# Turning quantised rows by DMA instead of TensorE in a Mamba block with a ternary MLP

## What is computed

```python
x = x + tanh(g_xattn[0]) * mamba(ctx_1024, z=layernorm(x), ...)
x = x + tanh(g_ffn[0]) * ffn(layernorm(x), w1, w2, w3)

def step(state, inp):                      # over the 512 rows, 512 channels x 16 states
    dA = exp(d[..., None] * A)
    state = state * dA + (d * u)[..., None] * b[:, None, :]
    return state, einsum('bdn,bn->bd', state, c)

def bitlinear(x, w):                       # w: -1, 0, 1 times a scale; x: 8-bit integers times a scale of the row
    xn = rmsnorm(x)
    return einsum('bsi,oi->bso', activation_quant(xn), weight_quant(w))

h = silu(bitlinear(x, w1)) * bitlinear(x, w2)      # 2048 wide
out = bitlinear(h, w3)
```

## Time and profile before

| | us |
|---|---|
| median of 3 executions | 655.52 |
| lowest, highest | 654.02, 656.09 |
| the profiled execution, its own time | 653.69 |
| its span (first to last instruction) | 651.9 |
| busy: POOL, DVE, ACT, PE, PEld | 587.9, 583.0, 530.7, 488.3, 296.4 |
| time of the 16 DMA engines in the SP queue's packets | 33.9% |

### The profile page before, as it was taken

The page is one execution under the profiler, slowest core; times in us unless marked ns, Lnnn a source line. Parts: engine busy times, 40 slices in busy tenths (PEclk is TensorE's granted clock), DMA queues, the critical chain, the costliest instruction groups (busy, mean ns, idle before and its releaser), DMA issues.

```text
span 651.9 us, 7928 instructions
## 1 busy us (share of the span) xinstructions
PE 488.3 (75%) x2560; PEld 296.4 (45%) x2560; DVE 583.0 (89%) x772; ACT 530.7 (81%) x969; POOL 587.9 (90%) x289
## 2 busy tenths in 40 slices
PE   8798878994564678777666486778676887668987
PEld 3254434552553445455534354455454554345543
DVE  6779779997998899999999999989997999999765
ACT  5764767788999778987798797899999898897675
POOL 1399999998999999999999999999999999999431
PEclk9988999997555979999786889889989897978999
DMA  5598587579960100147420100037700000000001
GB/s 186 193 407 309 183 329 276 198 270 389 374 262 0 39 1 2 47 153 276 132 78 0 33 2 17 1 127 244 254 37 1 17 1 18 0 16 18 1 17 48
DMA packets 24472, 80.77 MB, mean 124 GB/s; under 512 B 2464, under 2 KB 5152, under 8 KB 21360
## 3 DMA queue, kind: packets, MB, share of 16 engines
q1 hardware_dynamic: 24432, 80.27, 33.9%
HBM read 72.53 MB, written 7.73 MB: 123 GB/s over the span
## 4 chain that ended last, share of the span: by engine, by line
POOL 30%; DVE 29%; ACT 14%; issue 13%; PE 11%; DMA 2%; SPq 0%; DVEq 0%; POOLq 0%; ACTq 0%
POOL hh L708 15%; POOL hh L818 14%; DVE hh L773 9%; DVE hh L770 8%; DVE room L1048 4%; ACT da L736 3%; DVE sm L1093 2%; PE bank_a L1020 2%; PE bank_b L1029 2%; PE bank_y L851 2%; ACT room L1041 1%; PE da L1211 1%; DVE bank_y L576 1%; DVE sm L904 1%; ACT gbuf L922 1%
## 5 line engine op out<-in xcount | busy, mean ns | idle before, releaser
L773 DVE TENSOR_TENSOR_SCAN hh<-da,hh 128x1024 f32<-128x1024 f32 x85 | 193.4, 2280 | 3.1 <-ACT da L743 3.0
L851 PE MATMUL bank_y<-ident,hh 128*128 128x128 f32 x1024 | 145.3, 292 | 10.8 <-POOL hh L818 8.8
L851 PEld LDWEIGHTS bank_y<-ident,hh 128*128 128x128 f32 x1024 | 129.6, 152 | 40.1 <-issue 17.5
L813 POOL TENSOR_TENSOR hh<-hh,cc 128x1024 f32<-128x1024 f32 x60 | 141.0, 2350 | 0.2 <-ACT hl L756 0.2
L818 POOL TENSOR_TENSOR hh<-hh,cc 128x1024 f32<-128x1024 f32 x57 | 134.2, 2355 | 0.0
L708 POOL TENSOR_TENSOR hh<-pair,bb 128x1024 f32<-128x1024 f32 x30 | 70.5, 2352 | 26.4 <-DMA bb<-xd_scratch 24.2
L770 DVE TENSOR_TENSOR_SCAN hh<-da,hl,hh 128x256 f32<-128x256 f32 x128 | 85.4, 729 | 0.0
L708 POOL TENSOR_TENSOR hh<-wq,bb 128x1024 f32<-128x1024 f32 x32 | 75.3, 2357 | 1.8 <-PE bank_y L851 1.8
L702 POOL TENSOR_TENSOR hh<-wq,bb 128x1024 f32<-128x1024 f32 x32 | 75.1, 2346 | 0.3 <-PE bank_y L851 0.3
L702 POOL TENSOR_TENSOR hh<-pair,bb 128x1024 f32<-128x1024 f32 x32 | 75.2, 2355 | 0.0
L736 ACT ACTIVATE da<-wq,cst 128x256 f32<-128x256 f32 x128 | 53.3, 463 | 12.0 <-DVE hh L770 11.6
(11 more groups left out here) (271 smaller groups left out, 1051.7 us busy)
## 6 DMA issues: line engine op xcount, KB each, us to landing
bb<-xd_scratch SPq DMA_DIRECT2D x32, 512.0 KB, 5.1
cc<-xd_scratch SPq DMA_DIRECT2D x32, 512.0 KB, 6.9
wq<-weights SPq DMA_DIRECT2D x12, 1024.0 KB, 6.5
stage<-weights SPq DMA_DIRECT2D x8, 1024.0 KB, 6.1
xin<-x SPq DMA_DIRECT2D x4, 1024.0 KB, 5.4
room<-weights SPq DMA_DIRECT2D x4, 1024.0 KB, 8.2
u_scratch<-wq SPq DMA_DIRECT2D x6, 512.0 KB, 3.0
wq<-x SPq DMA_DIRECT2D x2, 1024.0 KB, 18.8
```

The source lines that it names most:

```text
L773: ins = v.tensor_tensor_scan(to, da, h, 0.0, ALU.mult, ALU.add)
L813: ins = g_.tensor_tensor(quarters(flat(hh[k % NH])), quarters(flat(hh[k % NH])), cc[:, n:n + 4, t], ALU.mult)
L851: mm = pe.matmul(bank_y[:, (first + c) * P:(first + c + 1) * P], flat(hh[k % NH])[:, at:at + P], ident[:, :], start=False, stop=(s == STEP ...
```

## The change

Tiles 0 to 11 no longer turn h on TensorE. SP issues two transposing DMAs for a tile, from the 16-bit h straight to hqT, which is then read as f16 with the 1536 still in it. `out_tensor` begins with a product of one row: -1536 (as f16, in row 0 of `ones`) times the column sums of w3, and adds the 16 products onto it. The column sums are made once, in slot 36, by 16 products of a column of ones with w3 (`column_sums`) and copied by ACT (`column_sums_scalar`). Tiles 12 to 15 keep the old way. The core of the diff:

```diff
+SUMS = 36
+        ones16 = sb("ones16", [P, 1], F16)
+        hqT16 = view(room, 5120, 1024).bitcast(F16).rearrange("p (a b) -> p a b", a=KF)
+        w3sum = view(room, 6400, 256).bitcast(F16)[0:1, :]
+        offset = ones[0:1, 0:P // 2].bitcast(F16)
+        d_turn = [loads("turned_h_first"), loads("turned_h_second")]
+        def column_sums(pe):
+            pe.wait_ge(*WA.of(("sign", NW - 1)))
+            pe.wait_ge(*YV.of(("p", NE - 1)))
+            pe.wait_ge(*PV.of("ident16"))
+            for f in range(KF):
+                mm = pe.matmul(bank_t[0:1, :], ones16[:, :], w3q[:, f, :], start=(f == 0), stop=(f == KF - 1))
+            WP.did(mm, "columns")
+        def column_sums_scalar(act):
+            act.wait_ge(*WP.of("columns"))
+            WA.did(act.activation(w3sum, bank_t[0:1, :], ACT.Copy), "columns")
...
+        def by_dma(i):
+            return i < END - 1
...  # xt_tensor
             elif i == 0:
-                pe.wait_ge(*x_done(i))
-                pe.wait_ge(*PV.of("ident16"))
+                pe.wait_ge(*WA.of("columns"))
...
+        def turn_by_dma(sp, i):
+            for r in range(2):
+                sp.wait_ge(*MA.of(("hq", i, r)))
+                if r == 0 and i:
+                    sp.wait_ge(*MP.of(("o", i - 1)))
+                d_turn[r].did(sp.dma_start_transpose(hqT16[:, 8 * r:8 * r + 8, :], h16_at(i, r)), ("hqT", i, r))
...  # out_tensor
-            if i == 0:
-                pe.wait_ge(*WA.of(("sign", NW - 1)))
-            if i < END - 1:
-                pe.wait_ge(*MA.of(("hqT", i, 1)))
+            if by_dma(i) and 0 in groups:
+                pe.wait_ge(*ZA.of(("gT", max(j for j in range(NE, 4 * NE) if z_turn_slot(j) < turned(i) + 2))))
+                if tile_slot(i + 1) - 1 < turned(i) + 2:
+                    pe.wait_ge(*MA.of(("xqT", i + 1)))
+                pe.wait_ge(*WV.of("offset"))
+                pe.matmul(bank_g(i)[:, :], offset, w3sum, start=True, stop=False)
             for g in groups:
-                if i == LAST:
+                if by_dma(i):
+                    pe.wait_ge(*d_turn[g // 2].of(("hqT", i, g // 2)))
+                elif i == LAST:
...
-                    mm = pe.matmul(bank_g(i)[:, :], hqT[:, f, :], w3q[:, f, :], start=(f == 0), stop=(f == KF - 1))
+                    mm = pe.matmul(bank_g(i)[:, :], (hqT16 if by_dma(i) else hqT)[:, f, :], w3q[:, f, :],
+                                   start=(f == 0 and not by_dma(i)), stop=(f == KF - 1))
...  # SP, in the loop over k
                     for i in range(END - 1):
+                        if k == turned(i):
+                            turn_by_dma(sp, i)
                         if k == turned(i) + 3:
                             store_out(i)
...  # ACT: in slot 36, behind the softplus and ahead of xr_scalar
+                    if k == SUMS:
+                        column_sums_scalar(act)
...  # ACT and PE: hqt_scalar and ht_tensor of tiles 0 to 11 go, in both loops
-                    for i in range(END - 1):
-                        if k == tile_slot(i) + 9:
-                            hqt_scalar(act, i, 1)
-                    for i in range(END - 1):
-                        if k == tile_slot(i) + 8:
-                            hqt_scalar(act, i, 0)
...  # PE, in slot 36, behind sums
+                    if k == SUMS:
+                        column_sums(pe)
```

More of the change, by code:

```diff
@@ L643, in weight_mean @@
             WV.did(v.reciprocal(winv, wmean))
+            WV.did(v.memset(offset, -MAGIC16), "offset")
             v.wait_ge(*PA.of("gates"))
@@ L1154, in ht_tensor @@
             else:
-                pe.wait_ge(*(MG if at_end(i) or i == END - 1 and r else MA).of(("hq", i, r)))
+                pe.wait_ge(*(MG if at_end(i) or r else MA).of(("hq", i, r)))
                 if i >= END:
                     pe.wait_ge(*turned_by(i - 1, r).of(("hqT", i - 1, r)))
[L1158 to L1162, removed]
-                elif r:
[L1164 to L1168, removed]
+                elif r:
+                    pe.wait_ge(s_scan, ALL)
                 else:
@@ L1198, in out_tensor @@
         def out_tensor(pe, i, groups=range(NCH)):
-            if i == 0:
-                pe.wait_ge(*WA.of(("sign", NW - 1)))
             if i >= END and 0 in groups:
                 pe.wait_ge(*MV.of(("out", i - 1)))
-            if i < END - 1:
-                pe.wait_ge(*MA.of(("hqT", i, 1)))
+            if by_dma(i) and 0 in groups:
[4 more added lines that the diff above has]
+                pe.matmul(bank_g(i)[:, :], offset, w3sum, start=True, stop=False)
             for g in groups:
-                if i == LAST:
+                if by_dma(i):
+                    pe.wait_ge(*d_turn[g // 2].of(("hqT", i, g // 2)))
+                elif i == LAST:
                     pe.wait_ge(*turned_by(i, g).of(("hqT", i, g)))
-                elif i >= END - 1 and g % 2 == 0:
+                elif g % 2 == 0:
                     pe.wait_ge(*turned_by(i, g // 2).of(("hqT", i, g // 2)))
                 for f in range(4 * g, 4 * g + 4):
-                    mm = pe.matmul(bank_g(i)[:, :], hqT[:, f, :], w3q[:, f, :], start=(f == 0), stop=(f == KF - 1))
+                    mm = pe.matmul(bank_g(i)[:, :], (hqT16 if by_dma(i) else hqT)[:, f, :], w3q[:, f, :],
+                                   start=(f == 0 and not by_dma(i)), stop=(f == KF - 1))
             if g == NCH - 1:
@@ L1578, in _ @@
                             hq_scalar(act, i, 1)
[L1579 to L1584, removed]
                     for first, n, done in TURNS:
@@ L1692, in _ @@
                     for i in range(END - 1):
-                        if k == tile_slot(i) + 9:
-                            ht_tensor(pe, i, 1)
-                    for i in range(END - 1):
                         if k == tile_slot(i) + 10:
@@ L1700, in _ @@
                             z_turn_tensor(pe, i)
-                    for i in range(END - 1):
-                        if k == tile_slot(i) + 8:
-                            ht_tensor(pe, i, 0)
                     for n in PAIR:
@@ L1725, in _ @@
                             dt_proj(pe, 2 * n + 1)
[L1726 to L1731, removed]
                     for i in range(END - 1):
@@ L1806, in _ @@
                 v.wait_ge(*PG.of("ident"))
+                v.memset(ones16[:, :], 1.0)
                 PV.did(v.tensor_copy(ident16[:, :], ident[:, :]), "ident16")
```

## The result

| | before | after |
|---|---|---|
| median, us | 655.63 (4 runs) | 659.70 (4 runs) |
| ratio, with 95% interval | | 1.0069 (1.0047 to 1.0091) |
| the same once more, beside later kernels | 655.12 (23 runs) | 659.46 (6 runs), 1.0065 (1.0045 to 1.0085) |
| span of the profiled execution, us | 651.9 | 657.0 |

The account below looks back on a forecast made before the run. The prediction took POOL to set the pace, the other engines only having to be in time. It summed 653.69 + 0.8 (column sums) + 0.7 (transposing DMAs) = 655.2 us, on the medians 655.52 + 1.5 = 657.0 us, range 652.5 to 692.

Parts of the forecast that it names:

- the dear end of the column sums: Slot 36: with slow sums and slow turns the chain ends at 213.5 us and costs 2.6 us; ends 0 to 3.
- a late DMA: Tiles 2, 6 and 7: a transpose behind a 512 KB load is some 4.4 us later; 0.7 us entered, ends 0 and 4.
- the two DMA rivals: PE waits at L1211 for turned halves: 7.7 us a half, 683 us (chance 0.15); or 10 us a half, 728 us (0.15).
- the term of the column sums: Slot 36: the sums delay POOL's input product of slot 42 by 0.4 to 1.2 us; 0.8 us entered.
- What bounds the kernel: 198 to 604 us: POOL, busy 405.5 of 406.0 us, sets the pace; at most its 2.0 us of waits can be gained.
- The transposing DMAs: Tiles 0 to 11: a half takes 5.0 us, inside every deadline; 0.7 us entered for tiles turning beside loads.
- My dear end: Transposing DMAs: 1,024 rows of 256 bytes, each a packet of 0.121 us, make 7.7 us a half.
- The room of 1.8 us behind L1211: After tile 0's products: the next turns end at 260.55 us, POOL needs them at 262.31 us, so 1.8 us of lateness is covered.
- The one-row product: One more matmul of 512 columns a tile ahead of the products with w3: 0.23 us on PE, twelve times, cost 0.
- SP's stream: SP stops at two waits for h in slot 8, with only loads due slots later and stores behind them: cost 0.
- the removed work: ACT loses 24 copies, 26.4 us, and PE 192 turns, 15.0 us, all beside POOL's products: nothing gained.
- Faster: Rival, chance 0.10: ACT feeds DVE earlier, column sums stay hidden, POOL loses its remaining waits, at most 2.0 us: 653.5 us.

Follow-up runs that it names:

- e6: The kernel before with one more VectorE instruction of 2.28 us in slot 36, read by nobody: 657.62 us, ratio 1.0044 to the kernel before.
- e1: The changed kernel without the column sums and ACT's wait for them in slot 36 (w3sum cleared in slot 42): 655.27 us, ratio 0.9996 to the kernel before.
- e3: The changed kernel with the column sums moved from slot 36 to slot 42, ACT's copy behind z there: 654.94 us, ratio 0.9986 to the kernel before.

## Why the prediction was right or wrong

The measured 659.7 us lies in the range (652.5 to 692). The point (657.0, 1.5 us up) was 2.7 us short, and the likeliest outcome by my chances, within 0.3% at 0.48, was not what happened: 0.7% slower, which I gave 0.42. Of this 0.42 only 0.12 stood for the dear end of the column sums or a late DMA; 0.30 stood for the two DMA rivals, which did not come. So the range held the result with the help of a term that was nothing (0.7 us for the DMAs, ends 0 and 4), while the term of the column sums, 0.8 us with the ends 0 and 3, measured 4.1 us, beyond its own end.

**The step that failed** is the last sentence on the column sums: that DVE's delay of some 5 us "stays hidden and is worked off by the time saved on ACT". The delay itself was well put: 5.04 us by the trace, against "some 5". Its fate was not. I compared DVE's next state with the moment at which POOL needs it, found 8.2 us between them, and stopped. But DVE is busy for 73.7 of the 75 us from 230 us on, and of its 4.1 us of idle time ahead of them it won back 0.7. The lead itself is used up by the work of the coming slots: for POOL's product at 276.75 us DVE's state, of the recurrence at 272.17 us, is there by 2.3 us and no longer by 8.2. A lead that shrinks like this is no room, and time saved on ACT does not help an engine that doesn't wait for ACT, or waits for an ACT that is late by the same time. Nor does POOL need DVE only for states: it needs buffers, which PE frees behind products that wait for DVE's chunks. POOL lost 0.88 us at once and 3.5 us more from 258 to 280 us. e6 shows the step by itself: 2.28 us of VectorE there cost 2.2 us of POOL.

**What bounds the kernel.** "POOL sets the pace ... the other engines only have to be in time" was half of it. POOL's full rows allow no gain, and there was none clear of the noise (e1, e3, with ACT 22 us lighter). They say nothing on how near the others are to being late. Up to 280 us POOL is the bound together with the buffers that come to it by way of DVE and PE, at 274.4 us with 0.1 us to spare.

**The column sums.** The chain was right in every link, and nearly in size: the products 6.07 us (I took 5.26, bounds 3.62 to 6.7), ACT's copy 0.59 (0.7), the gap on POOL 0.88 us (0.8). That the gap near 211 us would be about 1 us was right, and it was the smaller part. The sign that I had set for this step, a gap there of up to 3 us, came out right for this reason although the step was wrong: it looked at 211 us alone. The sign that did speak was POOL's busy share from 215 to 600 us, 98.9% (380.69 of 385 us) where I asked for over 99%.

**The transposing DMAs.** 3.2 us a half where I took 5.0, bounds 2.0 and 7.7; 5.0 at most, in the loaded stretch. The 0.7 us that I entered is 0 as far as the medians tell. My dear end was wrong in one factor: the halves are moved as rows of 256 bytes, as I assumed (25,344 packets more on the queue, 1,056 a DMA), but a packet costs far less than the 0.121 us of the earlier trace rows. From the shares of the two pages, 0.393 x 16 x 657.0 less 0.339 x 16 x 651.9 us, divided by 25,344, it is 0.023 us. Both DMA rivals fall by that. The Trainium skill gives 1309 ns for one block of 128x128 by DMA (VectorE: DVE Perf Modes, The three transpose paths). My estimate from it, eight such blocks in a row in 10.5 us, falls too; no run here turned a single block. The Trainium skill's 261 GB/s (DMA: Bandwidth & Descriptors, Latency and other measured facts), which made 3.0 us for a half by my estimate, agrees with the 3.2 us measured.

The room of 1.8 us behind L1211, which I took from tile 0 for all tiles, was not needed; at 274.4 us POOL's buffer has 0.1 us.

**The one-row product, SP's stream, the removed work.** Each cost nothing, as said. ACT is 22 us less busy and not 26. The other sign, POOL's products of 2.35 us, must be read from start to start: their mean on record is 2.40 us in the changed kernel (L833), but near 330 us they follow one another every 2.31 us in both kernels. The one-row product stands 0.31 us ahead of the others (260.30 to 260.61). SP is held for 1.3 us by each transpose, and no wait of an engine is put down to that.

**Faster** did not come; e3, the change without its dear place, is 0.14% faster with 1 inside its interval.

## What to carry to other kernels

An engine that is busy without a gap sets a limit to what can be gained; it doesn't show how much the others may lose. Before calling a delay hidden, look at two things in the stretch behind it. The first is the delayed engine's own idle time: no more than that can be worked off, and less where the idle time ends with something that is itself late by the delay (of 4.1 us DVE won back 0.7). The second is the tightest handover to the engine that sets the pace, be it a state or a freed buffer: an engine that shows no wait can still be served with only 0.1 us to spare, and what has not been won back by then is the price. A small piece of work that is done once should be put where the engines around it wait anyway: here the same 16 products cost about 4 us in slot 36 and nothing six slots later.

## What the runs showed of the hardware that I had not expected

A transposing DMA from SBUF to SBUF of 128x1024 16-bit numbers lands in 3.2 us and holds the SP queue for 1.3 us to be issued (2.5 at most), four times the 0.32 us of an ordinary load there. Small packets of such a DMA are cheap, 0.023 us of an engine each for 256 bytes, by the estimate above. Two per tile, or four, beside loads of 512 KB, left no mark on the time of the kernel that the medians show.

The clock that PE is granted made the sums longer as well: 16 products of 512 columns took 6.07 us after 5.85 us of idling, at a mean granted clock of 0.59, and 3.62 us in slot 42 behind work of its own, at 1.00, the figure that two of the three products with w3 show. A part came back: the eight turns behind the sums took 1.04 us, where they took 1.92 in the kernel before.
